# A decoder layer on one core: x in two halves on two queues, and GpSimd's split of the cross keys and its bias sums moved into the self attention

## What is computed

```python
x = x + self_attn(layernorm(x))            # 16 heads of 64
x = x + cross_attn(layernorm(x), ctx_1024, mask)   # 16 heads of 8, 512 context rows
x = x + moe(layernorm(x))                  # 8 experts of 256, top 2, and a shared one
...
pattern = einsum('bhid,bhjd->bhij', k, q) * scale; prob = softmax(pattern, axis=-2)
out = einsum('bhis,bhid->bhsd', prob, v)   # then concat @ Wo + bo
```

## Time and profile before

| what | us |
|---|---|
| median of 3 runs | 216.43 (215.0 to 216.7) |
| the profiled execution, its own time | 216.21 |
| its span, first to last instruction | 214.4 |
| TensorE busy | 197.4 |
| VectorE busy | 163.5 |
| ScalarE busy | 127.7 |
| GpSimd busy | 91.8 |

### The profile page before, as it was taken

The page is one execution under the profiler, slowest core; times in us unless marked ns, Lnnn a source line. Parts: engine busy times, 40 slices in busy tenths (PEclk is TensorE's granted clock), DMA queues, the critical chain, the costliest instruction groups (busy, mean ns, idle before and its releaser), DMA issues.

```text
span 214.4 us, 4361 instructions
## 1 busy us (share of the span) xinstructions
PE 197.4 (92%) x1556; PEld 149.4 (70%) x1556; DVE 163.5 (76%) x429; ACT 127.7 (60%) x300; POOL 91.8 (43%) x133
## 2 busy tenths in 40 slices
PE   7699997999998996998788999999898999999993
PEld 7388775676765674665545576566576899999993
DVE  1778668877777995768999999998995677458753
ACT  2466457857574655356877989989596532362320
POOL 6599945664646747003999700000120003611422
PEclk9999999999999999699999999999999999999999
DMA  6960748999436115005102300000000000000000
GB/s 164 394 166 3 196 49 100 132 114 100 62 44 199 42 40 111 0 0 181 44 0 84 66 0 3 0 5 0 2 0 3 3 0 2 3 0 28 0 0 24
DMA packets 10732, 12.67 MB, mean 59 GB/s; under 512 B 864, under 2 KB 8544, under 8 KB 10640
## 3 DMA queue, kind: packets, MB, share of 16 engines
q1 hardware_dynamic: 10040, 11.41, 26.7%
q10 hardware_dynamic: 576, 0.80, 1.0%
q0 software_dynamic: 96, 0.20, 0.3%
HBM read 10.96 MB, written 1.44 MB: 58 GB/s over the span
## 4 chain that ended last, share of the span: by engine, by line
PE 74%; DVE 14%; issue 4%; ACT 3%; DMA 2%; POOL 2%; POOLq 0%; DVEq 0%
PE ps L845 12%; PE ps L807 9%; PE ps L736 7%; PE ps L751 7%; PE ps L866 7%; PE ps L723 6%; PE ps L785 6%; PE ps L640 5%; PE ps L767 5%; PE ps L653 4%; DVE q_t L1064 3%; DMA x_in<-in_x 2%; DVE x_hat L931 1%; PE ps L823 1%; DVE prob_t L1137 1%
## 5 line engine op out<-in xcount | busy, mean ns | idle before, releaser
L1064 DVE CUSTOM_DVE_ANT_0 q_t<-ps,mask_add 128x512 f32<-128x512 f32 x64 | 41.3, 682 | 2.2 <-PE ps L767 2.2
L445 POOL TENSOR_TENSOR prob<-prob,rec 128x512 f32<-128x512 f32 x32 | 32.6, 1041 | 23.3 <-DVE rec L1119 23.3
L545 ACT ACTIVATE prob<-ps,low 128x256 f32<-128x256 f32 x64 | 29.5, 475 | 18.4 <-DVE low L1054 18.4
L570 ACT ACTIVATE q_t<-q_t,low 128x512 f32<-128x512 f32 x44 | 29.4, 719 | 10.5 <-DVE low L1064 10.4
L384 POOL TENSOR_TENSOR rstd<-var_eps,minus_half 128x2 f32<-128x2 f32 (+1 forms) x5 | 3.9, 773 | 67.6 <-DVE var_eps L924 67.6
L807 PE MATMUL ps<-ident,q_t 128*128 128x128 f32 x176 | 23.4, 275 | 3.7 <-DVE place_o L1137 1.4
L807 PEld LDWEIGHTS ps<-ident,q_t 128*128 128x128 f32 x176 | 19.9, 141 | 8.9 <-issue 4.2
L1054 DVE TENSOR_REDUCE low<-ps 128x2 f32<-128x512 f32 x32 | 20.5, 682 | 6.3 <-PE ps L723 6.2
L555 ACT ACTIVATE q_t<-ps 128x512 f32<-128x512 f32 x18 | 10.6, 599 | 20.9 <-PE ps L845 20.9
L1134 DVE COPY prob_t<-ps 128x512 f32<-128x512 f32 x32 | 20.6, 681 | 3.0 <-PE ps L751 3.0
L767 PE MATMUL ps<-k_stack,q_stack 72*128 72x512 bf16 x64 | 19.1, 383 | 1.8 <-issue 1.8
(11 more groups left out here) (165 smaller groups left out, 419.9 us busy)
## 6 DMA issues: line engine op xcount, KB each, us to landing
k_stack<-k_dram SPq DMA_DIRECT2D x9, 256.0 KB
q_stack<-q_dram SPq DMA_DIRECT2D x6, 192.0 KB
wg<-in_L_ffn_w_gate SPq DMA_DIRECT2D x1, 1024.0 KB, 24.4
wu<-in_L_ffn_w_up SPq DMA_DIRECT2D x1, 1024.0 KB, 35.3
k_dram<-prob SPq DMA_DIRECT2D x1, 768.0 KB, 3.6
w_in<-in_L_attn_Wq ACTq DMA_DIRECT2D x2, 256.0 KB, 5.3
context<-in_ctx SPq DMA_DIRECT2D x1, 512.0 KB, 6.3
w_in<-in_L_attn_Wv SPq DMA_DIRECT2D x1, 512.0 KB, 7.2
```

Source lines behind the costliest of these rows:

```text
L445: nc.gpsimd.tensor_tensor(pr, pr, rec1[:, s % 2, r, :].unsqueeze(2).to_broadcast([P, C, S]), ALU.mult).then_inc(s_norm1, 1)
L545: e = nc.scalar.activation(prob1[:, s % 3, r, c * S:(c + 1) * S], ps[:, 2 * (s % 2) + r, c * S:(c + 1) * S], ACT.Exp, bias=low1[:, s % 2, ...
L570: nc.scalar.activation(prob2[n % 3][:, c, :], score2[n % 2][:, c, :], ACT.Exp, bias=low2[:, n % 2, c:c + 1], scale=-1.0).then_inc(s_exp2, 1)
L1064: nc.vector.tensor_tensor_reduce(out=score2[n % 2][:, c, :], in0=ps[:, 2 * (n % 2) + c, :], in1=mask_add[:, c, :], scale=1.0, scalar=3e38, ...
```

## The change

1. `x_in` is loaded in two DMAs of 128 KB: batch 0 as SP's first, batch 1 as ScalarE's first, ahead of its loads of `Wq` and the biases.
2. GpSimd's split of `k2_t`, four instructions on 128x1024 in the prologue, becomes eight instructions on 128x512, one in each of the steps g = 0 to 7, behind the division of that step. The first waits until all 21 items are issued, as `k2_parts` now lies in memory of its own use (it shared `prob1` before, and now shares that of `qk_parts`). `s_kparts` is raised at steps 3 and 7, and SP waits for both.
3. The sums `x + bo1` go to steps 8 and 9, `v2 + bv2` to steps 14 to 17.
4. The four banks of `values_of_tokens(1)` are used in another order, `values_evac(1)` comes in two pieces on ScalarE (one before `exp1(1)`, one behind it), and the first transposes (`turn1(0)`) wait for three of the four evacuations on each engine instead of four; the fourth is waited for by `values1(0)`. ScalarE's wait for `k2_dram` in `exp1(1)` goes away.
5. `WARM_UP` is 17 instead of 14.

```diff
-WARM_UP = 14
+WARM_UP = 17
...
-V_BANKS = (5, 6, 7, 4)
+V_BANKS = ((5, 6, 7, 4), (4, 5, 6, 7))
...
-            load(x_in[:, :, :], a["x"], d_x)
+            load(x_in[:, 0:C, :], a["x"][:, 0:C, :], d_x)
...
-            sp.wait_ge(s_kparts, 1)
+            sp.wait_ge(s_kparts, 2)
...
-            pool.wait_ge(s_ev["act"], evacuated(index_of("kx", 1))[1])
-            link(nc.gpsimd.tensor_copy(k2_parts[:, 0, :], k2_t))
-            link(nc.gpsimd.tensor_tensor(k2_rest, k2_t, k2_parts[:, 0, :], ALU.subtract))
-            link(nc.gpsimd.tensor_copy(k2_parts[:, 1, :], k2_rest))
-            nc.gpsimd.tensor_tensor(k2_parts[:, 2, :], k2_rest, k2_parts[:, 1, :], ALU.subtract).then_inc(s_kparts, 1)
-            pool.wait_ge(d_x, 16)
-            pool.wait_ge(d_bo, 48)
-            for c in range(NC_):
-                nc.gpsimd.tensor_tensor(x_bo[:, c, :], x_in[:, c, :], bo1[:, :], ALU.add).then_inc(s_xbo, 1)
+
+            def split_keys2(step):
+
+                half, part = divmod(step, 4)
+                cols = slice(half * BANK, (half + 1) * BANK)
+                full, rest_ = k2_t[:, cols], k2_rest[:, cols]
+                if step == 0:
+                    pool.wait_ge(s_ev["act"], evacuated(index_of("kx", 1))[1])
+                    pool.wait_ge(s_item, len(ITEMS))
+                if part == 0:
+                    link(nc.gpsimd.tensor_copy(k2_parts[:, 0, cols], full))
+                elif part == 1:
+                    link(nc.gpsimd.tensor_tensor(rest_, full, k2_parts[:, 0, cols], ALU.subtract))
+                elif part == 2:
+                    link(nc.gpsimd.tensor_copy(k2_parts[:, 1, cols], rest_))
+                else:
+                    nc.gpsimd.tensor_tensor(k2_parts[:, 2, cols], rest_, k2_parts[:, 1, cols], ALU.subtract
+                                            ).then_inc(s_kparts, 1)
...
                 if 1 <= g <= N_SELF:
                     divide1(g - 1)
+                if g < 8:
+                    split_keys2(g)
+                elif g < 8 + B:
+                    add_bo1(g - 8)
+                elif 14 <= g < 14 + KC:
+                    add_bv2(B * (g - 14), B)
...
+            act.dma_start(x_in[:, C:NC_, :], a["x"][:, C:NC_, :]).then_inc(d_x, 16)
             act.dma_start(wq1[:, 0:BANK], a["L0_attn_Wq"][:, 0:BANK]).then_inc(d_qk[0][0], 16)
...
-                    if s == 1 and r == 1:
-                        act.wait_ge(d_kdram, 16)
...
                 if g == 0:
-                    values_evac(g)
+                    values_evac(0, 0)
+                    values_evac(0, 1)
+                if g == 1:
+                    values_evac(1, 0)
                 for what in BETWEEN.get(g, ()):
                     between(what)
                 if g < N_SELF:
                     exp1(g)
                 if g == 1:
-                    values_evac(g)
+                    values_evac(1, 1)
...
-                    elif r == 0:
-                        pe.wait_ge(s_vev[0], NC_)
-                        pe.wait_ge(s_vev[1], NC_)
+                    else:
+                        pe.wait_ge(s_vev[r], 3)
```

More of the change, by code:

```diff
@@ L402, in _, with add_bo1 @@
             split(wv1, [wv1_parts[:, i, :] for i in range(2)]).then_inc(s_vparts, 1)
-            pool.wait_ge(s_ev["act"], evacuated(index_of("kx", 1))[1])
-            link(nc.gpsimd.tensor_copy(k2_parts[:, 0, :], k2_t))
-            link(nc.gpsimd.tensor_tensor(k2_rest, k2_t, k2_parts[:, 0, :], ALU.subtract))
-            link(nc.gpsimd.tensor_copy(k2_parts[:, 1, :], k2_rest))
-            nc.gpsimd.tensor_tensor(k2_parts[:, 2, :], k2_rest, k2_parts[:, 1, :], ALU.subtract).then_inc(s_kparts, 1)
-            pool.wait_ge(d_x, 16)
-            pool.wait_ge(d_bo, 48)
-            for c in range(NC_):
-                nc.gpsimd.tensor_tensor(x_bo[:, c, :], x_in[:, c, :], bo1[:, :], ALU.add).then_inc(s_xbo, 1)
+            def split_keys2(step):
[14 more added lines that the diff above has]
+                                            ).then_inc(s_kparts, 1)
+            def add_bo1(b):
+                pool.wait_ge(d_x, 32)
+                pool.wait_ge(d_bo, 48)
+                for c in range(b * C, (b + 1) * C):
+                    nc.gpsimd.tensor_tensor(x_bo[:, c, :], x_in[:, c, :], bo1[:, :], ALU.add).then_inc(s_xbo, 1)
             def split_tokens(b):
@@ L427, in split_weights, with add_bv2 @@
                 split((wg, wu)[which][:, e, :], [t[:, :] for t in w_parts[which][e]]).then_inc(s_wparts, 1)
[L430 to L433, removed]
+            def add_bv2(first, count):
+                pool.wait_ge(s_ev["act"], evacuated(index_of("vx", 1))[1])
+                pool.wait_ge(d_bo, 48)
+                for c in range(first, first + count):
+                    nc.gpsimd.tensor_tensor(v2[:, c, :, 0:HD2], v2[:, c, :, 0:HD2], bv2[:, :, :], ALU.add
+                                            ).then_inc(s_v2, 1)
             def add_bo2(b):
@@ L557, in silu_step, with values_evac @@
                     between(what)
[L559 to L563, removed]
+            def values_evac(g, chunk):
+                i = 2 * chunk
+                act.wait_ge(s_v, NC_ * g + i + 1)
+                nc.scalar.copy(v1[:, V_ITEMS[g][i][0], 0:BANK], ps[:, V_BANKS[g][i], :]).then_inc(s_vev[0], 1)
             def exp2(n):
@@ L732, in values1 @@
                     pe.wait_ge(s_o1, s)
+                else:
+                    pe.wait_ge(s_vev[0], NC_)
+                    pe.wait_ge(s_vev[1], NC_)
                 for c in range(C):
@@ L816, in values_of_tokens @@
                             pe.wait_ge(s_vparts, 1)
-                        engine, value = evacuated(max(j for j in range(len(ITEMS)) if j % 8 == V_BANKS[i]))
+                        engine, value = evacuated(max(j for j in range(len(ITEMS)) if j % 8 == V_BANKS[0][i]))
                         pe.wait_ge(s_ev[engine], value)
                     else:
-                        pe.wait_ge(s_vev[half], 2 * (g - 1) + i // 2 + 1)
+                        earlier = V_BANKS[0].index(V_BANKS[1][i])
+                        pe.wait_ge(s_vev[earlier % 2], earlier // 2 + 1)
                     for j, (xi, wi) in enumerate(BIG_PARTS):
-                        last = mm(ps[:, V_BANKS[i], :], xv_parts[:, xi, c * P:(c + 1) * P],
+                        last = mm(ps[:, V_BANKS[g][i], :], xv_parts[:, xi, c * P:(c + 1) * P],
                                   wv1_parts[:, wi, half * BANK:(half + 1) * BANK],
@@ L933, in normalise @@
                 ins.then_inc(s_xhat, 1)
-            dve.wait_ge(d_x, 16)
+            dve.wait_ge(d_x, 32)
             statistics(0, x_in, 0, NC_)
@@ L1067, in low_scores2, with values_evac @@
                                                    ).then_inc(s_low2, 1)
[L1069 to L1073, removed]
+            def values_evac(g, chunk):
+                i = 2 * chunk + 1
+                dve.wait_ge(s_v, NC_ * g + i + 1)
+                nc.vector.tensor_copy(v1[:, V_ITEMS[g][i][0], BANK:2 * BANK], ps[:, V_BANKS[g][i], :]
+                                      ).then_inc(s_vev[1], 1)
             def bank_y(i):
```

2 lines of the change are left out of this document (1 added, 1 removed).

## The result

The changed kernel takes 240.51 us (median of 4 runs, 239.15 to 241.4) against 215.72 us (214.52 to 216.7): a ratio of 1.115, with a 95% interval of 1.105 to 1.124. It is 11.5% slower. The profiled execution took 239.68 us, with a span of 237.8 us.

A forecast was written before the change was run, and what follows sets the result against it. TensorE, busy 197.4 of 214.4 us, was taken as the bound, with the keys' split delaying it through SP's queue. The profiled 216.2 + 24.9 us (the prologue's 0.6 included) gave 241.1 us, range 235.0 to 243.8.

The forecast's parts named there:

- Keys' split: GpSimd, steps 0 to 7: pieces fit 1.56 us of idle time; the last ends at 52.7, 31.25 us later.
- The hold travels with `k_stack`: SP's queue: SP is free 42.1 us after the first load of `k_stack`, the queue empty 45.9 us after it.
- Rival 3: SP's queue: the 22 us hold may come from experts' weights or self attention, not the keys; 215.6 us; chance 0.05.
- Rival 2: SP's queue: the hold shortens by the 3.5 us gap before `wg`; 237.6 us, with rival 1 233.9; chance 0.06.
- `q_dram` behind the backlog: SP's queue: `q_dram` is served behind the weights flowing until 101.65, then 2.0 us to `q_stack`; 24.9 us in all.
- rival 1: SP's queue: the queries wait only for SP, not for the backlog; 237.4 us; chance 0.14.
- Cross scores: TensorE starts them at 101.65 + 2.0 + 6.99 = 110.6 instead of 85.71.
- Prologue: Start of the kernel: 0.6 us gained, with 0.5 taken for x in halves and 0.1 for the first transposes.
- Clock: TensorE after the wait: one stretch at 1.2 GHz already paid, none added; one more, 1.7 us, as the bound.

The follow-up runs named there:

- experiment 1: The changed kernel with the keys' split back in the prologue, `k2_parts` in `prob1` and ScalarE's wait for `k2_dram`: 214.29 us, ratio 0.997 to the kernel before.
- experiment 2: The changed kernel with the queries' DMAs of batch 0 ahead of the experts' weights in SP's queue: 234.32 us, ratio 1.088 to the kernel before.
- experiment 4: The changed kernel with `k_stack` in three loads of 24 partitions, `q_stack` in nine of 8: 226.61 us, ratio 1.053 to the kernel before.
- experiment 3: The changed kernel with the queries' DMAs of batch 0 issued by ScalarE at step 14: 242.38 us, ratio 1.126 to the kernel before.
- experiment 7: The kernel before with only x in halves on two queues and the warm-up of 17: 214.48 us against 214.48, ratio 0.999.
- experiment 8: The kernel before with only the bias sums in the steps and the new order of the values' banks and copies: 214.88 us against 214.48, ratio 1.002.
- experiment 9: The variant of experiment 1 with ScalarE's scaling of the queries' bias behind its first casts: 213.66 us, ratio 0.996 to the kernel before.

## Why the prediction was right

The forecast was 241.1 us in a range of 235.0 to 243.8; measured 240.5. By its steps:

- *Keys' split.* Forecast for its end 52.7 less 0.6; measured 51.7 (`k_dram` at 51.72). GpSimd's pieces sat in its idle time as said, and TensorE's step stayed, but not everywhere by the margin that I had read from one row: in the shorter early steps a piece ended at 38.51 and the division behind it followed with no idle time. That cost nothing; the first output projection began at 38.58, in experiment 1, without the pieces, at 38.62. GpSimd's timeline after, for the last piece, answers to the earlier trace rows:

```profile
48.54 2.04 POOL L462 TENSOR_TENSOR prob<-prob,rec 128x512 f32<-128x512 f32 x2 [1.01 <-DVE rec L1146]
50.54 1.16 POOL L419 TENSOR_TENSOR k_parts<-context,k_parts 128x512 bf16<-128x512 f32 x1
52.08 2.04 POOL L462 TENSOR_TENSOR prob<-prob,rec 128x512 f32<-128x512 f32 x2 [0.38 <-DVE rec L1146]
```

- *The hold travels with `k_stack`.* Forecast 42.1 us from the first load to a free SP, measured 40.3; queue empty after 45.9, measured 45.7 (101 - 55.3, by a stretch that ends there). Rival 3, that the hold isn't the keys', is refuted by SP's timeline of the changed kernel, and experiments 2 and 4 name the keys. Rival 2, the gap before `wg`, is true for SP's freedom by up to 1.8 us and of no effect, since the empty queue decides.
- *`q_dram` behind the backlog.* I took 2.0 us after the queue had emptied, and it landed 0.5 us after 101. This term was 1.5 us too large: 2.07 us is what the whole DMA takes in an empty queue, but behind a backlog its own data are the tail of it. That the wait is for the backlog is right (rival 1 would have had it landed at 97.7). My argument, however, rested on SP's timeline, and SP's program order is not the main thing: in experiment 2 SP was free, and in experiment 3 another queue was used, and the landing came at 96.30 and 98.69 all the same.
- *Cross scores.* Forecast 110.6, measured 108.28. Terms: 1.5 us of the landing, 0.65 of the queue's emptying (101 for 101.65, in it the prologue's 0.4), 0.2 of the queries' 6.99 us (6.80 measured).
- *Prologue.* Forecast 0.6 us; the changed kernel's profile has the three-part matmuls 0.9 us earlier and the first output projection 1.1 us. Alone, over twelve executions each, neither part is a gain that shows (experiments 7 and 8). Together, in experiment 1, the medians are 0.5 us apart, inside an interval that holds 0 too. The 0.6 us are thus neither confirmed nor refuted. If one sorts the executions afterwards and keeps those with a granted clock of 0.997 or more, experiment 1 lies 0.7 us below the kernel before (medians of 7 and 13, 213.91 and 214.61), experiment 9 lies 0.8 below, experiment 8 0.1 below, and experiment 7 level. What I missed was the landing of the biases; I had priced the added issue at 0.4 us of ScalarE's queue, not at the 1.0 to 2.3 us by which the biases landed later.
- *Clock.* I counted no more than the one slow stretch of before, with one more as the bound. TensorE was at the 1.2 GHz level from about 87 on, through the wait and until 111.4, and a second time from 125.4:

```profile
125.40:127.60 2.20, 2.20 (x10) 1.82 (x11) 2.14 (x6) 1.14 (x3) 2.04 (x5) 0.50 0.04 12
```

That stretch stands where the cross attention runs, and what follows the start of the cross scores is 129.5 us long against 128.7. The first stretch cost as much as in the kernel before: from the cross scores to the third output projection pass 8.7 us in both.

The start of the cross scores was forecast 2.3 us too late, what follows it 0.8 us too short, and so the profiled execution (239.68) lies 1.4 us below the forecast. That the median of the runs lies within 0.6 us of it is in part luck.

## What to carry to other kernels

Before moving a producer into idle time, follow the DMA that it feeds, and then everything behind that DMA on the DMA engines: a transfer that holds half of them for 40 us may be free when it starts at 25 and cost 23 us when it starts at 55, though the engine that produces for it still has idle time. Read how much slack there is from the end (here the cross scores' start less 53 us: the keys had to start by about 31), not from the idle share of the engine that receives the work. When an early load is cut in two over queues, look at what else is queued on the second one and who waits for that.

## What the runs showed of the hardware

- A DMA on another, empty queue was no faster past a backlog: 21.83 us on ScalarE's queue, 20.5 us behind the keys on SP's, 2.07 us with nothing in flight. In both cases about half of its data moved well before the keys were through, and nearly all of the other half only as the keys ended (from 91.5 on in experiment 2, from 94 on in experiment 3).
- 2.36 MB into 8 partitions at a time keep later DMAs waiting for 40 us; the same bytes into 24 partitions at a time free SP after 19.2 us. The keys' packets of 32 KB took 4.1 us each in the first form (79 to 91.5 of experiment 2), and the earliest of them 3.5 us against 2.2 in the second.
- Before the cross scores TensorE waited 1.76 us in the profile of the kernel before and 1.59 in that of experiment 1, and both have a stretch at the 1.2 GHz level behind it; in those of experiments 7, 8 and 9 it waited 1.23, 1.42 and 1.29 us and the clock was at full speed throughout. Their spans are 212.7, 212.1 and 211.9 us against 214.4 and 213.3. The 29 executions of the kernel before beside experiment 7 fall apart by the same number: with a mean granted clock of 0.997 or more they took 214.04 to 214.92 us (19 of them), with 0.984 to 0.992 they took 215.12 to 217.07. A difference of 1 us between single profiles of this kernel can come from there.
